# A graph and expert layer on one core: the edge columns split 112, 176, 256, 256, and fewer unread products

## The reference

```python
n = layernorm(x)                                   # 6250 x 256
agg = segment_sum(n[dst], src); cnt = segment_sum(1, src)
x = x + n @ W1.T + b1 + (agg / max(cnt, 1)) @ W2.T + b2
z = layernorm(x); g = z @ Wg.T + bg                # 8 gates, the best 2, softmax
x = x + sum over the 2 experts e of p_e * (relu(z @ W1[e].T + b1[e]) @ W2[e].T + b2[e])
```

## Time and profile before

| what | value |
|---|---|
| median of the runs | 1919.41 us |
| the profiled execution, its own time | 1919.03 us |
| its span | 1916.9 us |
| TensorE busy | 1756.7 us, 92% |
| POOL busy | 1142.0 us, 60% |
| ScalarE busy | 1117.4 us, 58% |
| VectorE busy | 965.0 us, 50% |
| mean granted clock of TensorE | 0.981 |

### The profile page before, as it was taken

How to read it: one execution, slowest core, us unless ns; L and a number is a source line. 1 busy time by engine, 2 the same in 40 slices (tenths; PEclk the granted TensorE clock), 3 DMA queues, 4 the chain that set the end, 5 groups by cost and what they waited for, 6 DMA issues and landing times.

```text
span 1916.9 us, 41498 instructions
## 1 busy us (share of the span) xinstructions
PE 1756.7 (92%) x11167; PEld 1487.4 (78%) x11167; DVE 965.0 (50%) x2320; ACT 1117.4 (58%) x3316; POOL 1142.0 (60%) x1141
## 2 busy tenths in 40 slices
PE   5888999799987899877888889999999999999997
PEld 4655885588765677656666779999999999999997
DVE  6868877899667888533335877111111111111111
ACT  4964776477654899755652767444444444444443
POOL 1167777776777777777777734445445445454453
PEclk9989999999989999999999999999999999999999
DMA  9333333333333333344544867643443424242421
GB/s 314 101 93 106 100 98 104 106 103 97 101 103 107 106 106 105 107 139 138 144 136 124 272 214 250 176 102 65 124 94 71 127 38 126 36 128 36 129 36 18
DMA packets 113112, 224.31 MB, mean 117 GB/s; under 512 B 27286, under 2 KB 76604, under 8 KB 107094
## 3 DMA queue, kind: packets, MB, share of 16 engines
q0 software_dynamic: 61152, 129.45, 27.3%
q1 hardware_dynamic: 32576, 74.98, 11.5%
q10 hardware_dynamic: 19254, 18.32, 3.0%
HBM read 371.77 MB, written 34.91 MB: 212 GB/s over the span
## 4 chain that ended last, share of the span: by engine, by line
PE 56%; POOL 20%; issue 10%; DVE 7%; DMA 4%; ACT 1%; SPq 1%; DVEq 1%; POOLq 0%; ACTq 0%
POOL arena L652 20%; PE bank L1317 19%; PE bank L1333 19%; PE bank L1282 8%; PE bank L1057 5%; DMA arena<-ytab,arena 2%; DVE agg L1959 1%; PE bank L1305 1%; PE bank L1257 1%; PE bank L1103 1%; DVE arena L1439 1%; DMA gw<-in_gw2t 1%; DMA ytab<-arena 1%; DVE arena L1441 1%; DVE arena L1408 1%
## 5 line engine op out<-in xcount | busy, mean ns | idle before, releaser
L652 POOL DMA_INDIRECT arena<-ytab,arena x784 | 749.2, 956 | 254.8 <-issue 219.7
L1282 PE MATMUL bank<-arena 128*128 x2356 | 622.9, 391 | 76.0 <-SPq L527 70.9
L950 ACT ACTIVATE arena<-bank,agg 128x128 f32<-128x128 f32 x840 | 308.7, 368 | 402.6 <-PE bank L1317 344.8
L1282 PEld LDWEIGHTS bank<-arena 128*128 128x128 f32 x2356 | 412.0, 195 | 168.9 <-issue 106.2
L1317 PEld LDWEIGHTS bank<-arena,agg 128*128 128x128 f32 x3360 | 392.1, 192 | 6.0 <-issue 1.1
L1317 PE MATMUL bank<-arena,agg 128*128 128x128 f32 x3360 | 393.7, 276 | 0.7 <-issue 0.7
L1333 PE MATMUL bank<-agg,arena 128*128 128x256 f32 x1680 | 380.1, 379 | 0.4 <-DMA agg<-in_b 0.4
L1959 DVE TENSOR_TENSOR agg<-agg,bank 128x257 f32 x589 | 247.3, 420 | 260.4 <-PE bank L1282 216.4
L685 POOL DMA_INDIRECT out<-arena x105 | 171.1, 1629 | 324.3 <-issue 235.1
L1333 PEld LDWEIGHTS bank<-agg,arena 128*128 128x128 f32 x1680 | 311.0, 190 | 38.6 <-DMA agg<-in_b 0.7
L796 ACT ACTIVATE arena<-lanes,arena 128x128 f16<-128x128 f16 x816 | 247.9, 386 | 16.4 <-DVEq L1584 16.4
(11 more groups left out here) (284 smaller groups left out, 1658.6 us busy)
## 6 DMA issues: line engine op xcount, KB each, us to landing
agg<-in_w SPq DMA_DIRECT2D x210, 1024.0 KB
agg<-in_b SPq DMA_DIRECT2D x105, 128.0 KB
arena<-ytab,arena POOLq DMA_INDIRECT x784
ytab<-arena SPq DMA_DIRECT2D x12, 512.0 KB, 3.2
arena<-in_xt ACTq DMA_DIRECT2D x24, 256.0 KB, 2.9
node<-in_x SPq DMA_DIRECT2D x6, 896.0 KB, 12.3
agg<-in_xt SPq DMA_DIRECT2D x6, 896.0 KB, 12.9
out<-node ACTq DMA_DIRECT2D x6, 896.0 KB
```

What stands on the lines that cost most here:

```text
L652: pool.indirect_dma_start(out=rows[:, v % RU, h, 0:D], out_offset=None, in_=ytab[:, :], in_offset=bass.IndirectOffsetOnAxis(ap=rowidx[g % ...
L950: act.activation(hT[:, m, :], hidden_bank(j, m)[:, 0:T], ACT.Relu, bias=b1b[:, b, m:m + 1]).then_inc(s_fr, 1)
L1282: mm = pe.matmul(bank[bank_of(n)][:, 0:W], onehot[n // QUAD % 2][:, n % QUAD, h, :], pair[:, h * W:(h + 1) * W], start=(h == 0), stop=(h = ...
```

## The change

Two edits. The groups have 112, 176, 256 and 256 columns instead of 128, 176, 240 and 256. And the unread product is left out in the segments of groups 0 and 1 in which TensorE places the next group's columns.

```diff
-COLS = [128, 176, 240, 256]
+COLS = [112, 176, 256, 256]
...
-                    kept_busy(bank_of(n))
+                    if not (g < 2 and PLACE[g][0] <= k - FAR < PLACE[g][1]):
+                        kept_busy(bank_of(n))
```

## The result

The changed kernel takes 1928.12 us (median of five runs, 1925.60 to 1928.58), beside 1919.41 for the kernel before on the same chip (five runs too, 1916.98 to 1919.63): a ratio of 1.0048, 95% interval 1.0036 to 1.0060. It is slower by 8.7 us. The forecast was 1924.5 (+5.1), its own range 1921.5 to 1928, the 8-in-10 range 1918.5 to 1929.5; the measured time lies 0.1 us above the first and inside the second. The profiled execution took 1928.51 us, its span is 1926.8.

What follows compares the result with a forecast made beforehand. Up to 1110 us it took as bounds the first gather, then TensorE and VectorE until group 2's list, then POOL's gathers. The terms -5.2 - 9.9 + 2.6 + 17.6 = +5.1 gave 1924.5 us, own range 1921.5 to 1928.

Steps and rivals of the forecast that it cites:

- Three terms, in order: Time up to 1110 us: first gather, then TensorE and VectorE work until group 2's list, then POOL's gathers; the rest untouched.
- The first gather, -5.2: Before POOL's first gather: two fewer group 0 tiles on VectorE and narrower compares save 5.2 us; 3.5 if y's store holds it.
- Group 0, -9.9: From group 0's first gather to group 1's: fewer ranking and placing segments save 9.9 us, between 8 and 13.
- Ranking, -3.9: While group 1 is ranked beside group 0: 29 segments become 25 at 0.98 us each, saving 3.9 us.
- Placing, -6.0: Placing group 1 beside group 0: 46 segments instead of 50, VectorE setting 1.51 us each, saving 6.0 us.
- Group 1, +2.6: Group 1's gathers to group 2's: rank step and count tile +1.8, placing +0.6, first segments 0.2; between +1 and +7.
- Groups 2 and 3, +17.6: Stretch bound by POOL in groups 2 and 3: 14 more gathers at 1.26 us add 17.6 us.
- A: Rival: TensorE alone sets both placings, 1.44 us a segment in group 0; 1920.0 us, no change; chance 0.30.
- B: Rival: POOL's gathers bind groups 0 and 1 too once TensorE is relieved; -20.5, 1899 us; chance 0.06.
- C: Rival: TensorE's granted clock stays low or falls again in the placings, about 2.5 us each; 1929 us and up; chance 0.06.
- D: Rival: leaving out the product saves no 0.11 us, weight loads stand bare, placing segments stay as long; 1932 us; chance 0.06.
- Gather at 103.5, 156 us, 227 us, 629 us, last near 1115: POOL's forecast timeline: first gather at 103.5, group 1's 156 us later, group 2's 227 after, 629 to the last near 1115.

## Why the prediction was nearly right, and what was off

**Three terms, in order.** Right. The span grew by 9.9 us and the last gather came 9.05 later; 0.85 lies behind it.

**The first gather, -5.2.** Right: -5.8 (102.96), and -5.3 in the kernel with the columns alone. y didn't hold it.

**Group 0, -9.9. This is the step that failed: it gave 6.1.** Its parts, from the pairs' starts in both kernels:

- To the first pair and over the first 15 segments, forecast at nothing: +0.6 and +0.4. The +0.6 is of the profiled execution only; the kernels with the same front show 6.9 us there, as before.
- Ranking, -3.9: it gave 2.8. I priced a plain segment at what TensorE takes for it, 0.98, and the rank step at the other 1.53. But TensorE wasn't alone there, and the kernel before showed it: 0.59 of the 1.53 us is a wait for VectorE's L1439, between 158.11 and 158.70 us. Its sum there, from 134 to 181 us (total, times, longest):

```profile
PE bank L1032 <- DVE arena L1439: 3.7, 7, 0.6
```

  In the changed kernel VectorE is busy for as long as TensorE is:

```profile
134.00:175.00 41.00, 36.73 (x174) 25.45 (x174) 36.96 (x72) 18.57 (x46) 30.50 (x34) 0.96 0.36 104
```

  36.96 of 41.00 us, against 36.73 for TensorE. The four segments removed were worth 0.7 each, and the changed kernel without any product shows the same thing from TensorE's side: its products hide there. The clock of 0.96 isn't the reason: with the columns alone it was 1.00 in this window, and the 29 segments took 47.3 us beside 47.4. That VectorE's work is what sets this stretch is argued from these rows; no run adds to it there.
- Placing, -6.0: it gave 4.3. VectorE as the bound was right, and its own need of 1.51 too (54.5/36 = 1.51). What was wrong is that the slower engine's need was taken as the pace. Besides the pauses between sums VectorE stood still for some 1.9 us in 36 segments, 0.8 of it for TensorE, and TensorE for 1.9 us behind L807. TensorE's own need was mis-sized too: 1.47 and not 1.44, since its pair takes 0.91 us without the product ahead of it, not 0.87. So with needs of 1.51 and 1.47 each waited for the other, and the pace was 1.566. Over 46 segments that is 2.6 us too many; 1.7 were missing in the stretch, so its two ends gained 0.9 that I hadn't counted. For group 1 I had allowed for just this, for group 0 not. And of the 46 products the forecast had 2.5 us gained, where the kernel with the columns alone shows 0.8 at most.

**Group 1, +2.6.** It was +3.3. Placing took 1.734 us a segment (56 in 97.1 us), forecast 1.75, and before 1.741; so the products did pay for the sixteen columns there. Ranking and counting cost 2.0 (1.8). The first six segments of the placing cost 1.5 (21.25 us after 19.74) instead of 0.2, though in five kernels with these columns they vary from 20.2 to 21.9; the others gave 0.4 back, where +0.6 had been allowed.

**Groups 2 and 3, +17.6.** +17.7.

**Sum.** -5.8 - 6.1 + 3.3 + 17.7 = +9.1, where -5.2 - 9.9 + 2.6 + 17.6 = +5.1. Of the 4.0 us, 3.8 are group 0's.

**The rivals.** A (TensorE alone sets both): wrong in group 0 (1.566, not 1.44), as the extra operation for VectorE shows, and even TensorE's own need was 1.47; its 1.73 for group 1 was the better number. B (POOL the bound): wrong here, with 22 us over POOL alone in group 0; but with the old columns and the product left out it comes within 3 to 5 us of being the bound. C named nearly the measured time, 1929 us, for the wrong cause: in the middle of both placings the granted clock was 1.00 in spite of TensorE's short waits (0.56 us the longest), over group 0's first five segments of placing 0.78 before and 0.78 after the change (15.8 and 15.6 us), and products put back gained nothing. D: wrong as to segments that stay as long, but right in part: a product was worth its whole 0.11 us in group 1, and only 0.08 in group 0 (1.58 to 1.50 us with eight products, 1.43 to 1.35 with six).

**Signs named beforehand.** Gather at 103.5, 156 us, 227 us, 629 us, last near 1115: measured 102.96, 159.6, 227.6, 628.6 and 1118.79. VectorE's waits for TensorE nearly gone: yes (0.8 us). TensorE idle for 4 or 5%: 3.4%. POOL's waits longer: yes.

## What to carry to other kernels

Where one engine issues work group by group and the list of the next group is made beside this one, price each group as the larger of the issuer's time and the other engines' work, and never by one of them alone: moving work to a group pays only until the other side is the larger there. When an engine is relieved and a second one has nearly the same need, don't take the slower one's need as the pace; here 1.51 and 1.47 us made 1.566, and TensorE's gaps all stood where it takes over one-hots from a third engine, ScalarE, that had waited for VectorE. When a step is priced from a trace, look for waits inside it: they belong to another engine and don't go when this one is relieved. A filler instruction should be tried without, stretch by stretch: this one had a price in two of the four groups, and no use clear of the scatter in any.

## What the runs showed of the hardware that wasn't expected

- A lower granted clock of TensorE in groups 2 and 3 (0.95 against 0.97 to 0.99 over 600 us) changed nothing of the time, because POOL's gathers bound it.
- An extra VectorE operation of 128 f32 columns lasts 0.28 us and costs 0.20, since the next starts before its end.
- On VectorE a sum of 257 columns lasts 0.42 us. A tile's first step starts 0.33 us after it (210.72 and 211.05 us in the changed kernel), another sum only 0.62 us after it (213.03 and 213.65), with 0.20 us idle put down to the first sum. The kernel has each sum wait for the semaphore of the sum before it (`v.wait_ge(s_sum, n)`), and a tile's step not, so the pause may be the price of that wait; no run leaves it out. Twelve such pairs are the 2.4 us of L1960 behind L1960 in 36 segments, more than TensorE's whole idle time there.
